# ScalarE instead of VectorE rounds the last four gelu tiles of each round of the second layer

## The chip, the cores and the metric

The kernel runs on one core of one Trainium2 chip. The metric is the time of one execution on the device in microseconds (us), lower is better. The kernel before was timed three times: median 1027.67 us, 1027.58 to 1029.29.

## The reference

Two layers work on x, (4, 512, 128) in fp32. The first one (a normalisation, a test-time-training attention of 16 heads and a mixture of 16 experts) is not touched by the change. The second one is, cut to what matters:

```
xn = layernorm(x)                               # 4 batches of 512 tokens, 128 wide
s  = q k^T / sqrt(8); e = exp(s - max(s))       # attention, 16 heads of 8, 512 x 512 each
att = (e v / sum(e)) Wo^T + bo
cur = xn
for r in range(4):                              # the mixture, four rounds one after the other
    cw  = softmax over the top 2 of (cur Wg[r] + bg[r])        # weights of 4 experts
    hmid = gelu(cur W1 + b1)                    # per expert 128 -> 512
    cur = cur + sum_e cw_e * (hmid_e W2_e + b2_e)
x = x + att + cur
```

The matrix products of the mixture keep nearly the precision of fp32: each factor is split into a high part, rounded to a shorter float format (fp32r in the profile's names), and a low part, the rest. A product is then three matmuls: high x high, low x high, high x low.

## The kernel before

Tokens of one batch are columns: a tile is 128 features x 512 tokens. The second layer runs 16 rounds, numbered R = 0 to 15 here; R = 4 i + r, i the batch and r the round of its mixture. Each round also computes four of the batch's sixteen attention heads, so that TensorE has attention work between the steps of the mixture.

Every engine has one program, in an order written out by hand; `then_inc` on an instruction counts a semaphore up and `wait_ge` makes an engine wait for a count. An engine runs its instructions strictly in that order, so whatever stands behind a waiting instruction waits too. In a round (`round_` of each engine):

TensorE: `scores(t)` (L1410) makes the attention scores of 128 keys, 4 heads, into four PSUM banks; `logits` (L1429) the gate's; `hidden(0)` to `hidden(15)` the 16 hidden tiles (4 experts x 4), three matmuls each by the helper `mm3` (L1117 to L1119); `outputs(0)` to `outputs(15)`, three matmuls each with the same helper, multiply the split gelu tiles by W2, four tiles to an expert, and the last of an expert counts `outputs_ready`; `turned(t)` (L1420) makes the scores again, turned and less their maximum, for the exp; `values(t)` (L1379) multiplies the exps with v. The end of the order is: outputs(0), (1), the turned maxima (L1484), outputs(2), (3), turned(0), outputs(4) to (6), turned(1), outputs(7), (8), values(0), turned(2), outputs(9), (10), values(1), turned(3), outputs(11) to (15), values(2), values(3). `turned(1)` needs exp 0 to be done, since both use the same four banks, and so on.

ScalarE: 16 gelus (L611), with a few small steps between them; then four exps (L626), one behind each `turned`; then one Copy of the heads' values (L597). Gelu and exp need a table load (ACT_TABLE_LOAD) between them. A gelu from the ninth on waits until the tile whose place it takes has been split: there are places for eight.

GpSimd splits tiles 0 to 11 (`POOL_TILES = 12`): L1088 rounds a tile (`hdh`), L1090 subtracts the rounded one from it (`hdl`).

VectorE: maxima of the scores (L933), gate arithmetic, then the stretch that the change touches, with what each step waits for:

```
expert(0)      # waits for outputs_ready of expert 0; L949 scales and weights, L955 adds to cur
split(12)      # L940 rounds by a multiply with ones, L943 subtracts
split(13)
expert(1)
split(14)
split(15)
expert(2)      # for r = 0 and i > 0 the division of the last batch's attention comes first
expert(3)
```

and at the start of the next round the split of `cur` (L959, L960), which its hidden tiles read. The split tiles lie in a ring of 12 places. Tile 12 takes the place of tile 0, so whoever writes `hdh` or `hdl` of tiles 12 to 15 must wait until expert 0's outputs of the same round are done (`outputs_ready`, L939 and, in the new program, on ScalarE too).

Of the kernel before, what the change touches and what calls it, by code (L numbers as in the profile page):

```python
# [7 lines left out]
ALU = mybir.AluOpType  # L8
ACT = mybir.ActivationFunctionType
AX_X = mybir.AxisListType.X  # L10

P = 128
B, S = 4, 512
# [11 lines left out]
E1, F1, R1 = 4, 512, 4  # L25
NF = F1 // P
# [37 lines left out]
def build(nc, A, out, const_d, dbg=None):  # L64
    with ExitStack() as ctx:
        def sb(name, shape, dt=F32):
            return ctx.enter_context(nc.sbuf_tensor(name, shape, dt))

        def sem(name):
            return ctx.enter_context(nc.semaphore(name))  # L70
# [116 lines left out]
        def sb(name, shape, dt=F32):  # L187
# [4 lines left out]
        RING = 3 * NF  # L192
        hdl = sb("hdl", [P, RING, S], F32R)
        hdh = sb("hdh", [P, RING, S], F32R)
        hd = [xn[:, :, :].rearrange("p (k t) d -> p k (t d)", k=4), sb("hd", [P, 4, S])]
        tile = lambda n: hd[n % 2][:, n % 8 // 2, :]
        W2h = sb("W2h", [P, E1, F1], F32R)
        W2l = sb("W2l", [P, E1, F1], F32R)
        W1r = ex[:, :, :, :].rearrange("p a q s -> p (a q) s")[:, 0:4, :]
        W2r = ex[:, :, :, :].rearrange("p a q s -> p (a q) s")[:, 4:8, :]  # L200
        W1h = sb("W1h", [P, E1, F1], F32R)
        W1l = sb("W1l", [P, E1, F1], F32R)
# [29 lines left out]
        ones2 = sb("ones2", [P, 2 * NT * E1])  # L232
# [14 lines left out]

        l2_norm_step, l2_squares = sem("l2_norm_step"), sem("l2_squares")
        xn2_turned, xn2_turned_taken, l2_w_turned, l2_w_taken, l2_w_split = sem("xn2_turned"), sem("xn2_turned_taken"), sem("l2_w_turned"), sem("l2_w_taken"), sem("l2_w_split")
        N_ROUNDS = ("xn_split", "w1_split", "w1_low", "w2_split", "pool_split", "dve_split", "cur_split", "rows_ready", "rows_high", "rows_low", "rows_placed", "v_ready", "v_taken", "scores_ready",  # L250
            "score_max", "maxima_split", "maxima_turned", "q_ready", "turned_ready", "exps_ready", "hidden_ready",
            "gelu_ready", "outputs_ready", "expert_scaled", "cur_added", "values_summed", "heads_taken", "heads_gathered", "sums_moved", "inverses_spread", "heads_divided",
            "logits_ready", "logits_taken", "logits_shifted", "gate_tanh", "gates_ready", "gates_turned", "gates_taken", "gates_stored",
            "gates_spread", "att_out", "result_ready", "result_stored")
        ROUND = {n: sem("rounds_" + n) for n in N_ROUNDS}
        moe_loaded = sem("moe_loaded")
# [158 lines left out]
        POOL_TILES = 12  # L415

        @block.scalar
        def _(act):
# [130 lines left out]
            n = 0  # L549
# [36 lines left out]
            def rows(i, k, bank_):  # L586
                n = 2 * i + 1 - k
                act.wait_ge(ROUND["rows_ready"], n + 1)
                if i:
                    act.wait_ge(ROUND["rows_placed"], 16 * 6 * R1 * i)  # L590
                act.activation(kqh[:, k, :], bank_[:, :], ACT.Copy).then_inc(ROUND["rows_high"], 1)

            def heads(R):
                act.wait_ge(ROUND["values_summed"], NT * (R + 1))
                if R:
                    act.wait_ge(ROUND["heads_gathered"], 32 * R)
                act.activation(ob[:, :], bank[5][:, :], ACT.Copy).then_inc(ROUND["heads_taken"], 1)  # L597

            def round_(R):
                i, r = divmod(R, R1)  # L600
                if R:
                    heads(R - 1)
                for n in range(E1 * NF):
                    act.wait_ge(ROUND["hidden_ready"], E1 * NF * R + n + 1)
                    if n >= 8:
                        act.wait_ge(ROUND["pool_split"], 2 * (POOL_TILES * R + n - 7))
                    elif R and n + 8 < POOL_TILES:
                        act.wait_ge(ROUND["pool_split"], 2 * (POOL_TILES * (R - 1) + n + 9))
                    elif R:
                        act.wait_ge(ROUND["dve_split"], 2 * ((E1 * NF - POOL_TILES) * (R - 1) + n + 9 - POOL_TILES))  # L610
                    act.activation(tile(n), bank[TILE_BANK[n % 3]][:, :], ACT.Gelu_apprx_tanh, bias=b1c[:, n:n + 1]).then_inc(ROUND["gelu_ready"], 1)  # L611
                    if n == 1:
                        act.wait_ge(ROUND["logits_shifted"], R + 1)
                        act.activation(half_tanh, gt[:, 0, :], ACT.Tanh, scale=0.5).then_inc(ROUND["gate_tanh"], 1)
                    if n == 7:
                        act.wait_ge(ROUND["gates_turned"], R + 1)
                        if R:
                            act.wait_ge(ROUND["gates_stored"], 16 * R)
                        act.activation(cwT[:, :], bank[7][0:E1 * NT, 0:P], ACT.Copy).then_inc(ROUND["gates_taken"], 1)
                    if n == 10 and r >= 2 and i + 1 < B:  # L620
                        rows(i + 1, 3 - r, bank[7])
                for t in range(NT):
                    act.wait_ge(ROUND["turned_ready"], NT * R + t + 1)
                    if NT * R + t >= 2:
                        act.wait_ge(ROUND["values_summed"], NT * R + t - 1)
                    act.activation(ex[:, t % 2, :, :], quad[:, :, :], ACT.Exp, scale=float(AD) ** -0.5).then_inc(ROUND["exps_ready"], 1)  # L626
# [3 lines left out]
            for R in range(B * R1):  # L630
                round_(R)
# [3 lines left out]
        def _(dve):  # L635
            n = [0]
# [261 lines left out]
            def round_(R):  # L898
# [34 lines left out]
                    dve.tensor_reduce(mx[:, t, :], quad[:, :, :], AX_X, ALU.max, negate=True).then_inc(ROUND["score_max"], 1)  # L933

                def split(n):
                    m = E1 * NF * R + n
                    dve.wait_ge(ROUND["gelu_ready"], m + 1)
                    if m >= RING:
                        dve.wait_ge(ROUND["outputs_ready"], (m - RING) // NF + 1)  # L939
                    dve.tensor_tensor(hdh[:, m % RING, :], tile(n), ones2[:, 0:1].broadcast_to([P, S]), ALU.mult).then_inc(ROUND["dve_split"], 1)  # L940
                    k = (E1 * NF - POOL_TILES) * R + n - POOL_TILES
                    dve.wait_ge(ROUND["dve_split"], 2 * k + 1)
                    dve.tensor_tensor(hdl[:, m % RING, :], tile(n), hdh[:, m % RING, :], ALU.subtract).then_inc(ROUND["dve_split"], 1)  # L943

                def expert(e):
# [34 lines left out]
                m = Mt[:, :, :].rearrange("p t (h c) -> p t h c", c=32)  # L980
# [3 lines left out]
                dve.tensor_tensor(qm[:, :], bank[7][:, :], qx[:, R % 2, :], ALU.add).then_inc(ROUND["q_ready"], 1)  # L984
                expert(0)
                split(12)
# [4 lines that stand above are left out]
                if r == 0 and i:  # L991
# [13 lines left out]
        def _(pool):  # L1005
# [70 lines left out]
            pool.memset(Mt[:, :, :], 0.0).then_inc(l2_pool_step, 1)  # L1076
            pool.memset(Vx[:, :, :, :], 0.0).then_inc(l2_pool_step, 1)
            pool.wait_ge(ROUND["w1_split"], 1)
            pool.tensor_tensor(W1l[:, :, :], W1r[:, :, :], W1h[:, :, :], ALU.subtract).then_inc(ROUND["w1_low"], 1)
            pool.wait_ge(ROUND["w2_split"], 1)  # L1080
            pool.tensor_tensor(W2l[:, :, :], W2r[:, :, :], W2h[:, :, :], ALU.subtract).then_inc(ROUND["w2_split"], 1)

# [24 lines left out]
        def _(pe):  # L1107
# [7 lines left out]
            def mm3(to, lh, ll, rh, rl, start=True, stop=True):  # L1115

                pe.matmul(to, lh, rh, start=start, stop=False, skip_group_check=True)  # L1117
                pe.matmul(to, ll, rh, start=False, stop=False, skip_group_check=True)  # L1118
                return pe.matmul(to, lh, rl, start=False, stop=stop, skip_group_check=True)  # L1119
# [199 lines left out]
            for b in range(B):  # L1319
# [3 lines left out]
                for g in range(E0 // 4):  # L1323
                    n = jobs[0]
# [68 lines left out]
            def round_(R):  # L1393
# [53 lines left out]
                def outputs(n):  # L1447
                    e, a = n // NF, n % NF
                    if a == 0 and e < 2:
                        pe.wait_ge(ROUND["gelu_ready"], E1 * NF * R + (14, 16)[e])  # L1450
                    if a == 0 and e >= 2:
                        pe.wait_ge(ROUND["expert_scaled"], E1 * R + e - 1)
                    m = E1 * NF * R + n
                    if n < POOL_TILES:
                        pe.wait_ge(ROUND["pool_split"], 2 * (POOL_TILES * R + n + 1))
                    else:
                        pe.wait_ge(ROUND["dve_split"], 2 * ((E1 * NF - POOL_TILES) * R + n - POOL_TILES + 1))
                    c = slice(a * P, (a + 1) * P)
                    last = mm3(bank[6 if e % 2 else 4][:, :], W2h[:, e, c], W2l[:, e, c], hdh[:, m % RING, :], hdl[:, m % RING, :], start=(a == 0), stop=(a == NF - 1))
                    if a == NF - 1:  # L1460
                        last.then_inc(ROUND["outputs_ready"], 1)
# [43 lines left out]
                if R == 0:  # L1505
                    pe.wait_ge(ROUND["w2_split"], 2)
                outputs(0), outputs(1)
                turn_maxima()
                outputs(2), outputs(3), turned(0), outputs(4), outputs(5), outputs(6), turned(1), outputs(7), outputs(8)
                values(R, 0), turned(2), outputs(9), outputs(10), values(R, 1), turned(3), outputs(11)  # L1510
                if R < LAST:
                    outputs(12), outputs(13), outputs(14), outputs(15), values(R, 2), values(R, 3)
# [3 lines left out]
            rows(0, 1, bank[1])  # L1516
            rows(0, 0, bank[0])
            pe.wait_ge(xn2_turned_taken, B)
            pe.wait_ge(ROUND["w1_low"], 1)
            for R in range(B * R1):  # L1520
                round_(R)
            attention_out(B - 1)
# [28 lines left out]
```

## Time and profile before

| | before |
|---|---|
| median of 3 runs | 1027.67 us |
| profiled execution | 1030.62 us |
| its span | 1028.7 us |
| TensorE busy | 929.5 us, 90% |
| VectorE busy | 832.1 us, 81% |
| GpSimd busy | 626.5 us, 61% |
| ScalarE busy | 557.7 us, 54% |

The span is the time from the first to the last instruction of the profiled execution. The second layer's rounds fill it from about 442 us to about 1010 us; one round is about 35 us. A line of the timeline gives start, duration, engine, line of the program, operation, output and input names, a count where several were merged, and in brackets the idle time of the engine just before it, with what ended it. Names: PE is TensorE, DVE VectorE, ACT ScalarE, POOL GpSimd; the x tiles `xn` and `hd` hold the gelus, `ex` the exps, `quad` is four PSUM banks.

### The profile page before, as it was taken

The numbers are of one execution on the slowest core, as the hardware profiler recorded it, in microseconds if no ns is written. First come the engines' busy times: TensorE is split into PE (matmuls) and PEld (weight loads), VectorE is DVE, ScalarE is ACT, GpSimd is POOL, SyncE is SP. The second block draws the span as 40 slices with busy tenths as digits, with TensorE's granted clock in tenths as the row PEclk, the third lists the DMA queues.
The fourth block names the chain that finished last, engine by engine and source line by source line (L and its number), as shares of the span: only waits on it lengthen the run. The fifth ranks groups of instructions, "written<-read, shape, count | busy, mean of one in ns | idle before, by whom it ended". The sixth has DMA issues, their size and how long they took to land.

```text
span 1028.7 us, 16635 instructions
## 1 busy us (share of the span) xinstructions
PE 929.5 (90%) x6216; PEld 651.3 (63%) x6216; DVE 832.1 (81%) x1276; ACT 557.7 (54%) x826; POOL 626.5 (61%) x575
## 2 busy tenths in 40 slices
PE   2688899999999789779999999999999999999993
PEld 1456678778787667755565566656656666566552
DVE  7778999998998752678888888888897888878882
ACT  3334555555555436254666565657656666666560
POOL 5464666666666300195966696678668766866690
PEclk9989999999999989989999999999999999999997
DMA  8000000000000030220110122011111111121010
GB/s 223 16 1 1 2 1 1 2 1 1 2 2 2 1 82 2 82 72 6 55 59 13 52 69 70 19 42 60 62 30 53 60 45 29 60 71 34 30 41 26
DMA packets 25006, 38.13 MB, mean 37 GB/s; under 512 B 9336, under 2 KB 15500, under 8 KB 22880
## 3 DMA queue, kind: packets, MB, share of 16 engines
q1 hardware_dynamic: 23296, 34.81, 11.2%
q10 hardware_dynamic: 1632, 2.27, 0.7%
q8 instruction: 50, 0.82, 0.3%
q14 instruction: 28, 0.23, 0.1%
HBM read 28.29 MB, written 1.44 MB: 29 GB/s over the span
## 4 chain that ended last, share of the span: by engine, by line
PE 54%; POOL 18%; DVE 13%; issue 8%; ACT 5%; DMA 1%; SPq 1%; POOLq 0%; ACTq 0%; DVEq 0%
POOL hdl L1090 10%; PE bank L1117 9%; PE bank L1119 7%; PE bank L1118 7%; PE quad L1158 5%; PE bank L1379 5%; POOL hdh L1088 4%; PE bank L1268 3%; PE quad L1243 3%; ACT ex L626 2%; PE quad L1152 2%; PE quad L1420 2%; PE quad L1315 1%; PE bank L1208 1%; PE bank L1350 1%
## 5 line engine op out<-in xcount | busy, mean ns | idle before, releaser
L933 DVE TENSOR_REDUCE mx<-quad 128x4 f32<-128x2048 f32 x64 | 146.3, 2286 | 40.1 <-PE quad L1410 40.0
L1088 POOL CAST hdh<-xn 128x512 fp32r<-128x512 f32 x96 | 66.3, 690 | 143.7 <-ACT xn L611 143.7
L626 ACT ACTIVATE ex<-quad 128x2048 f32<-128x2048 f32 x64 | 120.6, 1884 | 50.1 <-PE quad L1420 49.9
L1090 POOL TENSOR_TENSOR hdl<-hd,hdh 128x512 fp32r<-128x512 f32 x96 | 129.7, 1351 | 7.7
L1090 POOL TENSOR_TENSOR hdl<-xn,hdh 128x512 fp32r<-128x512 f32 x96 | 128.8, 1341 | 7.7
L611 ACT ACTIVATE hd<-bank,b1c 128x512 f32<-128x512 f32 x128 | 88.1, 688 | 64.0 <-POOL hdl L1090 33.5
L1117 PE MATMUL bank<-hdh,W2h 128*128 128x512 f32 x256 | 111.3, 435 | 2.7 <-DVE hdl L943 2.7
L611 ACT ACTIVATE xn<-bank,b1c 128x512 f32<-128x512 f32 x128 | 87.9, 687 | 34.3 <-POOL hdl L1090 19.5
L1119 PE MATMUL bank<-hdl,W2h 128*128 128x512 f32 x256 | 101.0, 395 | 0.0
L1118 PE MATMUL bank<-hdh,W2l 128*128 128x512 f32 x256 | 100.7, 393 | 0.0
L1117 PE MATMUL bank<-cH,W1h 128*128 128x512 f32 x192 | 81.2, 423 | 0.7 <-DVE cL L960 0.7
L1119 PE MATMUL bank<-cL,W1h 128*128 128x512 f32 x192 | 75.8, 395 | 0.0
L1118 PE MATMUL bank<-cH,W1l 128*128 128x512 f32 x192 | 75.6, 394 | 0.0
L1088 POOL CAST hdh<-hd 128x512 fp32r<-128x512 f32 x96 | 70.3, 732 | 0.0
L1117 PEld LDWEIGHTS bank<-hdh,W2h 128*128 128x128 f32 x256 | 48.0, 188 | 32.8 <-issue 11.4
L1158 PE MATMUL quad<-Wbd,arena 128*64 128x128 f32 x1024 | 67.3, 285 | 0.0
L1379 PE MATMUL bank<-ex,Vx 128*32 128x512 f32 x512 | 65.5, 605 | 0.0
L1049 POOL TENSOR_TENSOR arena<-arena,sm 128x512 f32<-128x512 f32 x32 | 33.4, 1044 | 52.1 <-DVE sm L774 52.1
L955 DVE TENSOR_TENSOR cur<-cur,add 128x512 f32<-128x512 f32 x60 | 62.2, 1036 | 2.1
L1158 PEld LDWEIGHTS quad<-Wbd,arena 128*64 128x64 f32 x1024 | 58.1, 142 | 6.8 <-issue 6.6
L1037 POOL TENSOR_TENSOR arena<-arena,gg 128x512 f32<-128x512 f32 x32 | 40.9, 1279 | 31.2 <-DVE arena L751 30.4
L949 DVE SCALAR_TENSOR_TENSOR add<-bank,b2T,cwB 128x512 f32<-128x512 f32 x64 | 47.7, 746 | 14.2 <-PE bank L1119 14.0
(295 smaller groups left out, 2275.4 us busy)
## 6 DMA issues: line engine op xcount, KB each, us to landing
cwB<-gate_rows SPq DMA_DIRECT2D x16, 1024.0 KB, 4.7
kx<-kqh SPq DMA_DIRECT2D x32, 64.0 KB, 2.1
qx<-kqh SPq DMA_DIRECT2D x32, 64.0 KB, 2.1
ex<-in_L_ffn_W SPq DMA_DIRECT2D x1, 1024.0 KB, 5.4
kx<-kql SPq DMA_DIRECT2D x16, 64.0 KB, 2.1
qx<-kql SPq DMA_DIRECT2D x16, 64.0 KB, 2.1
num<-ob SPq DMA_DIRECT2D x16, 64.0 KB
rec<-rec_rows SPq DMA_DIRECT2D x32, 32.0 KB, 2.1
```

The source lines that it names most:

```text
L611: act.activation(tile(n), bank[TILE_BANK[n % 3]][:, :], ACT.Gelu_apprx_tanh, bias=b1c[:, n:n + 1]).then_inc(ROUND["gelu_ready"], 1)
L626: act.activation(ex[:, t % 2, :, :], quad[:, :, :], ACT.Exp, scale=float(AD) ** -0.5).then_inc(ROUND["exps_ready"], 1)
L933: dve.tensor_reduce(mx[:, t, :], quad[:, :, :], AX_X, ALU.max, negate=True).then_inc(ROUND["score_max"], 1)
L949: dve.scalar_tensor_tensor(out=add[:, e % 2, :], in0=bank[6 if e % 2 else 4][:, :], scalar=b2T[:, e:e + 1], in1=cwB[:, e, :], op0=ALU.add, ...
L955: dve.tensor_tensor(now, before, add[:, e % 2, :], ALU.add).then_inc(ROUND["cur_added"], 1)
L1088: pool.tensor_copy(hdh[:, m % RING, :], tile(n)).then_inc(ROUND["pool_split"], 1)
L1090: pool.tensor_tensor(hdl[:, m % RING, :], tile(n), hdh[:, m % RING, :], ALU.subtract).then_inc(ROUND["pool_split"], 1)
L1117: pe.matmul(to, lh, rh, start=start, stop=False, skip_group_check=True)
L1118: pe.matmul(to, ll, rh, start=False, stop=False, skip_group_check=True)
L1119: return pe.matmul(to, lh, rl, start=False, stop=stop, skip_group_check=True)
L1158: last = pe.matmul(to[64 * k:64 * k + 64, a * P:(a + 1) * P], T[:, 4 * hf + a, 2 * g + k, :], Wbd[:, 2 * g + k, 4 * hf + a, :], start=Fals ...
L1379: last = pe.matmul(bank[5][32 * h:32 * h + 32, :], Vx[:, t, QH * r + h, :], ex[:, t % 2, h, :], start=(t == 0), stop=(t == NT - 1), skip_g ...
```

## The change

ScalarE gets a loop between its 16 gelus and its four exps, in which it rounds tiles 12 to 15 (an activation Copy into `hdh`) and counts a new semaphore, `act_high`. VectorE's `split` loses its multiply and waits for `act_high` instead; it only subtracts. `dve_split` therefore counts 1 per tile instead of 2, and the waits on it are divided by two. The semaphores `w1_low` and `w1_split` are made one, with the same order.

```
@@ ScalarE, round_ (the waits on dve_split, here and on TensorE, are halved) @@
+                for n in range(POOL_TILES, E1 * NF):
+                    m = E1 * NF * R + n
+                    act.wait_ge(ROUND["gelu_ready"], m + 1)
+                    if m >= RING:
+                        act.wait_ge(ROUND["outputs_ready"], (m - RING) // NF + 1)
+                    act.activation(hdh[:, m % RING, :], tile(n), ACT.Copy).then_inc(ROUND["act_high"], 1)
                 for t in range(NT):
                     act.wait_ge(ROUND["turned_ready"], NT * R + t + 1)
@@ VectorE, round_ @@
                 def split(n):
-                    m = E1 * NF * R + n
+                    m, k = E1 * NF * R + n, (E1 * NF - POOL_TILES) * R + n - POOL_TILES
                     dve.wait_ge(ROUND["gelu_ready"], m + 1)
                     if m >= RING:
                         dve.wait_ge(ROUND["outputs_ready"], (m - RING) // NF + 1)
-                    dve.tensor_tensor(hdh[:, m % RING, :], tile(n), ones2[:, 0:1].broadcast_to([P, S]), ALU.mult).then_inc(ROUND["dve_split"], 1)
-                    k = (E1 * NF - POOL_TILES) * R + n - POOL_TILES
-                    dve.wait_ge(ROUND["dve_split"], 2 * k + 1)
+                    dve.wait_ge(ROUND["act_high"], k + 1)
                     dve.tensor_tensor(hdl[:, m % RING, :], tile(n), hdh[:, m % RING, :], ALU.subtract).then_inc(ROUND["dve_split"], 1)
```

## Rows read from the trace of the kernel before

**Rows 1.** The page, its first part: busy time, share of the span, instructions.

```profile
PE 929.5 (90%) x6216; PEld 651.3 (63%) x6216; DVE 832.1 (81%) x1276; ACT 557.7 (54%) x826; POOL 626.5 (61%) x575
```

**Rows 2.** The page, the chain that ended last, by engine.

```profile
PE 54%; POOL 18%; DVE 13%; issue 8%; ACT 5%; DMA 1%; SPq 1%; POOLq 0%; ACTq 0%; DVEq 0%
```

**Rows 3.** The waits, TensorE from 400 us: us in total, times, longest.

```profile
PE quad L1420 <- ACT ex L626: 7.7, 9, 0.9
...
PE bank L1117 <- DVE hdl L943: 2.7, 3, 2.0
```

**Rows 4.** The timeline, ScalarE, round 7: last gelu to exp 0.

```profile
712.77 0.69 ACT L611 ACTIVATE hd<-bank,b1c 128x512 f32<-128x512 f32 x1 [1.24 <-POOL hdl L1090]
713.48 1.28 ACT L626 ACT_TABLE_LOAD   x1
714.77 1.88 ACT L626 ACTIVATE ex<-quad 128x2048 f32<-128x2048 f32 x1
```

**Rows 5.** The timeline, TensorE, round 7: turned(1), outputs(14), next hidden(0).

```profile
716.70 0.51 PE L1420 MATMUL quad<-qm,kx 32*128 32x512 f32 x4 [0.86 <-ACT ex L626]
...
725.36 0.39 PE L1117 MATMUL bank<-hdh,W2h 128*128 128x512 f32 x1
...
730.01 0.48 PE L1117 MATMUL bank<-xH,W1h 128*128 128x512 f32 x1
```

**Rows 6.** Groups of instructions: count, busy us, mean ns, idle before.

```profile
L940 DVE TENSOR_TENSOR hdh<-hd,ones 128x512 fp32r<-128x512 f32 x32 | 30.5, 952 | 0.0
...
L591 ACT ACTIVATE kqh<-bank 128x512 fp32r<-128x512 f32 x6 | 3.6, 600 | 3.8 <-PE bank L1119 3.8
...
L574 ACT ACTIVATE arena<-xn 128x512 f32<-128x512 f32 x4 | 2.5, 630 | 19.4 <-DVE xn L846 19.4
```

**Rows 7.** The timeline, VectorE, round 7: expert(0).

```profile
713.17 0.75 DVE L949 SCALAR_TENSOR_TENSOR add<-bank,b2T,cwB 128x512 f32<-128x512 f32 x1 [0.71 <-PE bank L1119]
```

**Rows 8.** The timeline, three engines, round 9.

```profile
784.70 1.28 ACT L626 ACT_TABLE_LOAD   x1
785.99 1.89 ACT L626 ACTIVATE ex<-quad 128x2048 f32<-128x2048 f32 x1
...
785.22 0.75 DVE L949 SCALAR_TENSOR_TENSOR add<-bank,b2T,cwB 128x512 f32<-128x512 f32 x1 [0.70 <-PE bank L1119]
...
787.93 0.51 PE L1420 MATMUL quad<-qm,kx 32*128 32x512 f32 x4
```

**Rows 9.** The timeline, three engines, round 8.

```profile
749.88 1.89 ACT L626 ACTIVATE ex<-quad 128x2048 f32<-128x2048 f32 x1 [0.62 <-PE quad L1420]
...
749.43 0.75 DVE L949 SCALAR_TENSOR_TENSOR add<-bank,b2T,cwB 128x512 f32<-128x512 f32 x1 [0.71 <-PE bank L1119]
...
747.36 0.63 PE L1484 MATMUL bank<-cst,Mt 128*128 128x128 f32 x4 [1.52 <-DVE Mt L982]
...
752.02 0.51 PE L1420 MATMUL quad<-qm,kx 32*128 32x512 f32 x4
...
766.75 0.48 PE L1117 MATMUL bank<-cH,W1h 128*128 128x512 f32 x1 [0.22 <-DVE cL L960]
```

**Rows 10.** The timeline, TensorE, round 0: turned(1), outputs(14), next hidden(0).

```profile
468.77 0.51 PE L1420 MATMUL quad<-qm,kx 32*128 32x512 f32 x4
...
479.57 0.53 PE L1117 MATMUL bank<-hdh,W2h 128*128 128x512 f32 x1 [1.99 <-DVE hdl L943]
...
486.07 0.49 PE L1117 MATMUL bank<-cH,W1h 128*128 128x512 f32 x1
```

**Rows 11.** The timeline, TensorE, first layer.

```profile
61.69 0.50 PE L1152 MATMUL quad<-Bhl,pair 4*128 4x512 f32 x1 [2.39 <-DVE arena L751]
```

**Rows 12.** Stretches, TensorE: us, busy (count), granted clock, DMA share, GB/s.

```profile
63.00:66.00 3.00, 3.00 (x26) 0.58 0.00 0
481.00:484.00 3.00, 3.00 (x15) 0.61 0.00 0
749.00:752.00 3.00, 3.00 (x15) 1.00 0.18 51
```

More of the change, by code:

```diff
@@ L249, in build @@
         xn2_turned, xn2_turned_taken, l2_w_turned, l2_w_taken, l2_w_split = sem("xn2_turned"), sem("xn2_turned_taken"), sem("l2_w_turned"), sem("l2_w_taken"), sem("l2_w_split")
-        N_ROUNDS = ("xn_split", "w1_split", "w1_low", "w2_split", "pool_split", "dve_split", "cur_split", "rows_ready", "rows_high", "rows_low", "rows_placed", "v_ready", "v_taken", "scores_ready",
+        N_ROUNDS = ("xn_split", "w1_split", "w2_split", "pool_split", "act_high", "dve_split", "cur_split", "rows_ready", "rows_high", "rows_low", "rows_placed", "v_ready", "v_taken", "scores_ready",
             "score_max", "maxima_split", "maxima_turned", "q_ready", "turned_ready", "exps_ready", "hidden_ready",
@@ L609, in round_ @@
                     elif R:
-                        act.wait_ge(ROUND["dve_split"], 2 * ((E1 * NF - POOL_TILES) * (R - 1) + n + 9 - POOL_TILES))
+                        act.wait_ge(ROUND["dve_split"], (E1 * NF - POOL_TILES) * (R - 1) + n + 9 - POOL_TILES)
                     act.activation(tile(n), bank[TILE_BANK[n % 3]][:, :], ACT.Gelu_apprx_tanh, bias=b1c[:, n:n + 1]).then_inc(ROUND["gelu_ready"], 1)
@@ L1078, in _ @@
             pool.wait_ge(ROUND["w1_split"], 1)
-            pool.tensor_tensor(W1l[:, :, :], W1r[:, :, :], W1h[:, :, :], ALU.subtract).then_inc(ROUND["w1_low"], 1)
+            pool.tensor_tensor(W1l[:, :, :], W1r[:, :, :], W1h[:, :, :], ALU.subtract).then_inc(ROUND["w1_split"], 1)
             pool.wait_ge(ROUND["w2_split"], 1)
@@ L1456, in outputs @@
                     else:
-                        pe.wait_ge(ROUND["dve_split"], 2 * ((E1 * NF - POOL_TILES) * R + n - POOL_TILES + 1))
+                        pe.wait_ge(ROUND["dve_split"], (E1 * NF - POOL_TILES) * R + n - POOL_TILES + 1)
                     c = slice(a * P, (a + 1) * P)
@@ L1518, in _ @@
             pe.wait_ge(xn2_turned_taken, B)
-            pe.wait_ge(ROUND["w1_low"], 1)
+            pe.wait_ge(ROUND["w1_split"], 2)
             for R in range(B * R1):
```

## The prediction

> **What bounds the kernel now.** I read the page first. TensorE is busy for 929.5 of the 1028.7 us [rows 1], and the chain that ended last lies on it for 54%, on GpSimd for 18%, on VectorE for 13%, on ScalarE for only 5% [rows 2]. So TensorE is the engine to lose time on; the 5% of ScalarE asks where its links of the chain sit, since the change gives work to exactly that engine. The table of waits answers it: from 400 us on, TensorE's matmuls of the second attention product (`turned`, L1420) stood 7.7 us in 9 waits of about 0.86 us for an exp, while its waits for VectorE's split tiles come to 2.7 us in all [rows 3]. VectorE's rounding, which the change takes away, hardly holds anything up; the exp does.
>
> Then I laid round 7 out by engine (16 rounds, 0 to 15; 9 of them, 1 to 3, 6, 7, 10, 11, 14 and 15, look alike). The last gelu runs from 712.77 to 713.46, the table load of exp follows at once, and exp 0 runs from 714.77 to 716.65 [rows 4]. TensorE has issued the outputs that it may and starts `turned(1)` at 716.70, 0.86 us late [rows 5]. From there it works without a listed idle to the first hidden tile of the next round at 730.01, which is 13.31 us [rows 5]. The gelus of that round wait for that tile, so a delay of exp 0 is not made good.
>
> **The change, part by part.** *Removed:* 4 multiplies (L940) a round on VectorE, 0.95 us each by their mean [rows 6], 3.8 us a round and 61 us over the kernel. VectorE is not what TensorE waits for here; this is worth nothing in the alike rounds.
>
> *Added, the copies:* 4 copies of 128x512 from SBUF to SBUF on ScalarE. The trace of before has no such Copy; the nearest is the Square of the same size between SBUF tiles, 0.63 us [rows 6]. Bounds: 0.60, a Copy of that size out of PSUM [rows 6], and 0.69, the gelu [rows 4]. I take 0.63, so 4 x 0.63 = 2.52 us. They stand behind the last gelu and ahead of the exps, so behind them queue the table load and the four exps, and behind those TensorE's `turned` and `values`.
>
> *Added, their waits:* the gelu they read is done. The other wait is for expert 0's outputs of this very round, `outputs(3)`. VectorE's L949 starts on the same event, at 713.17 [rows 7]: before the gelu ends at 713.46, so it costs nothing in the alike rounds. There exp 0 ends 2.52 later and TensorE's wait grows from 0.86 to 3.38: 9 x 2.52 = 22.7 us.
>
> In rounds 5, 9 and 13 the outputs are later. In round 9 the table load starts at 784.70 behind the last gelu and the exp at 785.99, but L949 only starts at 785.22, so the copies start then, 0.5 later than the load did [rows 8]. Exp 0 moves by 0.5 + 2.52 = 3.0. `turned(1)` at 787.93 followed exp 0's end (787.88) at once [rows 8], so all of it lands: 3 x 3.0 = 9.1 us.
>
> In rounds 4, 8 and 12 exp 0 waited for `turned(0)` and the table load lay under that wait. Round 8: the outputs at 749.43, then 2.52 of copies and 1.28 of load, so exp 0 at 753.2 where it was at 749.88, 3.3 later; `turned(1)` at 752.02 had 0.2 of room behind its end at 751.77 [rows 9], so it moves 3.1. But in these rounds the stretch from `turned(1)` to the next round's first hidden tile is 752.02 to 766.75, 14.73 us [rows 9], against 13.31 in round 7: VectorE was late, with the splits in its queue. Without the multiplies that 1.4 goes. Net 1.7; 3 x 1.7 = 5.1 us (round 8 stands for the three).
>
> Round 0 is such a one too: 17.30 us from 468.77 to 486.07 [rows 10], of which 4.0 can come back against 3.1 of delay: -0.9 us. I charge the other splits nothing: behind a TensorE that is 2.5 us later, VectorE's subtracts, fed by the copies from about 714.1, end well ahead of the outputs that read them. Sum: 22.7 + 9.1 + 5.1 - 0.9 = 36.0 us.
>
> *Added, the clock:* this is the second cost, and it comes from the length of the new stalls. After an idle of 1.99 us at 479.57 [rows 10], and of 2.39 us at 61.69 [rows 11], the granted clock of the stretches behind was 0.61 and 0.58, so mostly at 1.2 GHz; behind 1.52 us idle at 747.36 it stayed at 1.00, that is 2.4 GHz [rows 9, 12]. The 0.86 us of today does no harm; 3.0 to 3.4 us in every round are above every case that did. The price at a drop: from `outputs(14)` to the next hidden tile it took 479.57 to 486.07, 6.50 us, against 725.36 to 730.01, 4.65, in round 7 [rows 5, 10]: 1.85 us. Some of the slow time may fall into the stall itself and cost nothing, so I take 1.5, with 0 and 1.85 as ends: 16 x 1.5 = 24 us. The clock's slow stretch lies behind `turned(1)`, in TensorE's own work, and nothing covers it.
>
> The Trainium skill, "TensorE: Matmul & The Clock Gate" (§ The HAM clock gate), says that activity releases the throttle and that an engine idle for long enough falls back to the half rate; by its figures the stalls worked out here fall short of a full idle stretch, and the clock would stay up. The 1.99 us of round 0 already speaks against reading it so. By the skill's rule the sum is 36, by the rows 60.
>
> Total: 36 + 24 = 60 us. The profiled execution took 1030.62 us (span 1028.7), so it would be 1090.7; the median of the runs is 1027.67, 2.95 below the profiled one, and the forecast against it is 1088 us.
>
> **Rivals.**
> A. The clock stays up: the new stalls are single ones in dense work, and where the drops were seen it may have been something else in their neighbourhood that let the clock fall. For it: rows 11 and the first of rows 12 lie in the first layer, where TensorE is less busy. Against: 1.99 us in round 0 of this very loop was enough. 1027.7 + 36 = 1064 us.
> B. The drops last longer: a second slow stretch in each round, as the half rate makes TensorE late and further waits follow. 16 x 2 x 1.5 = 48 instead of 24: 1112 us.
> C. The other side, faster: ScalarE's share of the chain is small and VectorE's late splits are the true brake. Its place are the late stretches of rounds 0, 4, 8 and 12, its price 4.0 + 3 x 1.4 = 8.2 us, 1019 us. It decides only if exp 0 had 2.5 us of room ahead of `turned(1)`; the rows show 0.2 us in round 8 and none in 7 and 9.
> D. The delay is mostly absorbed (TensorE finds later work to catch up on): about 1040 us. Against it stands that 13.31 us hold no idle.
>
> **How the numbers follow.** Forecast 0.73, A 0.16, B 0.05, C 0.02, D 0.04. The forecast's own range is 1078 to 1096 (copies of 0.60 to 0.69 us: -2 to +4; drops of 1.0 to 1.85 each: -8 to +6; not all at their ends together). The 8 in 10 take in A: 1061 to 1097. This kernel's measurement tells about 0.2%, 2 us, from no change. Faster 0.02, within it 0.01, slower 0.97.
>
> **What would show it.** Of the new profile: 64 ScalarE copies of about 0.63 us between L611 and L626; TensorE's waits for L626 at `turned(1)` at about 3.4 us in most rounds, some 50 us in total instead of 7.7; the alike rounds 2.5 us longer without, about 4 with the clock; granted clock near 0.5 for some 3 us behind each such wait, so page digits of 8 or 9 where a 9 stood; VectorE's busy time down by about 61 us or more. The prediction is wrong if exp 0 starts 1.3 us behind the last gelu as today, if the waits are there but the clock holds (A), or if the alike rounds grow by more than 5 us (B).

## The result and the profile after

The changed kernel takes 1090.55 us (median of 4 runs, 1086.8 to 1091.3) against 1028.1 us of the kernel before: 1.060 times as long, interval 1.057 to 1.063. The forecast was 1088 us.

The lines that answer to [rows 1 to 3]: the page's busy times and its chain, and, from 400 us on, TensorE's waits (us in total, times, longest).

```profile
PE 952.7 (87%) x6216; PEld 661.8 (61%) x6216; DVE 760.8 (70%) x1212; ACT 591.4 (54%) x890; POOL 613.4 (56%) x575
```

```profile
PE 59%; POOL 14%; DVE 11%; ACT 10%; issue 4%; DMA 1%; SPq 1%; ACTq 0%; POOLq 0%; DVEq 0%
```

```profile
PE quad L1424 <- ACT ex L632: 46.5, 16, 3.1
```

VectorE is 71.3 us lighter (61 for the multiplies, most of the rest for its adds to `cur`, 0.83 us each by their mean where they were 1.04), and nothing is gained by it. ScalarE's share of the chain doubled. The wait at `turned` was 7.7 us in 9 places and is 46.5 us in 16. TensorE has the same 6216 matmuls as before and is busy 23.2 us longer with them, so they ran slower.

Round 7 on ScalarE, for [rows 4]:

```profile
737.64 0.69 ACT L611 ACTIVATE hd<-bank,b1c 128x512 f32<-128x512 f32 x1 [1.24 <-POOL hdl L1094]
738.23 0.62 ACT L627 ACTIVATE hdh<-xn 128x512 fp32r<-128x512 f32 x1
738.75 0.62 ACT L627 ACTIVATE hdh<-hd 128x512 fp32r<-128x512 f32 x1
739.27 0.62 ACT L627 ACTIVATE hdh<-xn 128x512 fp32r<-128x512 f32 x1
739.79 0.62 ACT L627 ACTIVATE hdh<-hd 128x512 fp32r<-128x512 f32 x1
740.43 1.28 ACT L632 ACT_TABLE_LOAD   x1
741.72 1.88 ACT L632 ACTIVATE ex<-quad 128x2048 f32<-128x2048 f32 x1
```

From the end of the last gelu (738.33) to exp 0 it is 3.39 us, where it was 1.31: 2.08 us more. The copies last 0.62 us each, but start 0.52 us apart, and the first starts 0.10 us before the gelu has ended. The same round on TensorE, for [rows 5], and its stretches (busy us, count, granted clock, DMA share, GB/s):

```profile
743.65 0.80 PE L1424 MATMUL quad<-qm,kx 32*128 32x512 f32 x4 [2.92 <-ACT ex L632]
...
749.11 0.80 PE L1424 MATMUL quad<-qm,kx 32*128 32x512 f32 x4
...
759.67 0.48 PE L1121 MATMUL bank<-xH,W1h 128*128 128x512 f32 x1
```

```profile
740.00:743.00 3.00, 0.73 (x4) 1.00 0.00 0
743.00:746.00 3.00, 2.35 (x8) 0.50 0.00 0
746.00:749.00 3.00, 3.00 (x12) 0.50 0.00 0
749.00:752.00 3.00, 3.00 (x22) 0.86 0.00 0
```

`turned(1)` waits 2.92 us, and behind it the clock is at half, 1.2 GHz, for some six microseconds. From `turned(1)` to the next hidden tile it is 16.02 us instead of 13.31. Not all rounds are like that: against the 13.3 us that this stretch takes at full clock, eight lose about 1.5 us, six (3, 4, 7, 8, 10 and 15, the last by its length beside experiment 1) about 2.7, and two, 12 and 13, nothing. Round 12, `turned(1)` and the next hidden tile, 13.32 us apart, and the stretch behind the idle:

```profile
942.18 0.51 PE L1424 MATMUL quad<-qm,kx 32*128 32x512 f32 x4 [2.82 <-ACT ex L632]
...
955.50 0.48 PE L1121 MATMUL bank<-cH,W1h 128*128 128x512 f32 x1
```

```profile
942.00:948.00 6.00, 5.82 (x36) 1.00 0.00 0
```

### The profile page after: what moved, and what is told of

Read it like the earlier page. It is cut to its first block, busy times and chain, and to the rows that moved or that the text cites. A ratio compares the mean times of both kernels' runs of the same rounds, so it can differ in the third digit from the quotient of the medians.

```text
span 1089.3 us, 16699 instructions
## 1 busy us (share of the span) xinstructions
PE 952.7 (87%) x6216; PEld 661.8 (61%) x6216; DVE 760.8 (70%) x1212; ACT 591.4 (54%) x890; POOL 613.4 (56%) x575
## 4 chain that ended last, share of the span: by engine, by line
PE 59%; POOL 14%; DVE 11%; ACT 10%; issue 4%; DMA 1%; SPq 1%; ACTq 0%; POOLq 0%; DVEq 0%
PE bank L1121 10%; POOL hdl L1094 9%; PE bank L1123 8%; PE bank L1122 8%; PE bank L1383 6%; PE quad L1162 5%; POOL hdh L1092 4%; ACT ex L632 3%; PE bank L1272 3%; ACT hdh L627 2%; PE quad L1424 2%; PE quad L1247 2%; ACT L632 2%; PE quad L1156 2%; PE bank L1212 1%
## 5 line engine op out<-in xcount | busy, mean ns | idle before, releaser
L1094 POOL TENSOR_TENSOR hdl<-hd,hdh 128x512 fp32r<-128x512 f32 x96 | 127.3, 1326 | 7.7
L1094 POOL TENSOR_TENSOR hdl<-xn,hdh 128x512 fp32r<-128x512 f32 x96 | 125.6, 1309 | 7.7
L1121 PE MATMUL bank<-hdh,W2h 128*128 128x512 f32 x256 | 116.8, 456 | 0.0
L1123 PE MATMUL bank<-hdl,W2h 128*128 128x512 f32 x256 | 106.6, 416 | 0.0
L1122 PE MATMUL bank<-hdh,W2l 128*128 128x512 f32 x256 | 106.4, 415 | 0.0
L611 ACT ACTIVATE xn<-bank,b1c 128x512 f32<-128x512 f32 x128 | 87.9, 687 | 32.7 <-POOL hdl L1094 19.4
L1424 PE MATMUL quad<-qm,kx 32*128 32x512 f32 x256 | 37.1, 570 | 46.5 <-ACT ex L632 46.5
L1383 PE MATMUL bank<-ex,Vx 128*32 128x512 f32 x512 | 72.7, 665 | 0.0
L1424 PEld LDWEIGHTS quad<-qm,kx 32*128 32x128 f32 x256 | 13.8, 206 | 93.2 <-ACT ex L632 68.4
L1121 PEld LDWEIGHTS bank<-hdh,W2h 128*128 128x128 f32 x256 | 51.1, 200 | 31.4 <-issue 17.9
L1092 POOL CAST hdh<-hd 128x512 fp32r<-128x512 f32 x96 | 64.8, 675 | 0.0
L1053 POOL TENSOR_TENSOR arena<-arena,sm 128x512 f32<-128x512 f32 x32 | 33.4, 1044 | 52.1 <-DVE sm L780 52.1
```

The lines of the kernel that those rows point to most:

```text
L1092: pool.tensor_copy(hdh[:, m % RING, :], tile(n)).then_inc(ROUND["pool_split"], 1)
L1094: pool.tensor_tensor(hdl[:, m % RING, :], tile(n), hdh[:, m % RING, :], ALU.subtract).then_inc(ROUND["pool_split"], 1)
L1383: last = pe.matmul(bank[5][32 * h:32 * h + 32, :], Vx[:, t, QH * r + h, :], ex[:, t % 2, h, :], start=(t == 0), stop=(t == NT - 1), skip_g ...
L1424: last = pe.matmul(quad[:, h, :], kx[rows_, R % 2, t * P:(t + 1) * P], qm[rows_, :], start=True, stop=True)
```

## The experiments

Seven kernels, each timed four times or five; one execution of each is profiled. In the table "loop" is the span of the profiled execution less the start of the first gelu, since the part ahead of it, which nothing here touches, differs by up to 3 us from run to run (442.45 to 445.5).

| | median us | ratio to before (interval) | loop us |
|---|---|---|---|
| before | 1028 to 1029 | 1 | 583.95 |
| changed | 1090.55 | 1.060 (1.057 to 1.063) | 643.80 |
| fillers in the stall | 1060.81 | 1.032 (1.031 to 1.034) | 616.65 |
| copies added, nothing removed | 1088.44 | 1.059 (1.057 to 1.062) | 640.93 |
| multiplies removed, no copies | 1022.42 | 0.995 (0.994 to 0.997) | 577.16 |
| copies between the exps | 1022.91 | 0.995 (0.993 to 0.997) | 577.40 |
| one copy ahead of the exps | 1037.29 | 1.008 (1.006 to 1.010) | 591.2 |
| two copies | 1060.11 | 1.030 (1.026 to 1.033) | 614.8 |
| three copies | 1071.91 | 1.041 (1.038 to 1.044) | 627.4 |

**1. Is it the idle that lets the clock fall?** TensorE gets work for the stall.

```
+                def filler():
+                    for k in range(10):
+                        pe.matmul(bank[7][:, :], W1h[:, 0, 0:P], high, start=True, stop=True, skip_group_check=True)
...
-                outputs(2), outputs(3), turned(0), outputs(4), outputs(5), outputs(6), turned(1), outputs(7), outputs(8)
+                outputs(2), outputs(3), turned(0), outputs(4), outputs(5), outputs(6), filler(), turned(1), outputs(7), outputs(8)
```

> The changed kernel, with ten more matmuls (512 columns each) on TensorE just ahead of turned(1), into a PSUM bank that nobody reads before it is written anew. Ten of them take about 2.2 us at the pace of 0.22-0.23 us in the rows, less than the 2.8 to 3.1 us for which TensorE waits there in the changed kernel, so they delay nothing and leave an idle of some 0.7 us. Theory (the idle stretch lets the clock fall, and the half clock behind it is the second cost): granted clock 1.00 through the rounds, and the time falls by the sum of the excess of the stretches from turned(1) to the next hidden tile, about 29 us: 1062 us (1058 to 1066). Rival (the clock falls for another cause, or the long stretches come from VectorE's and ScalarE's new order): stays at 1088 to 1091 us.

It took 1060.81 us. Round 7 of it, and the stretch around the fillers:

```profile
725.79 2.50 PE L1479 MATMUL bank<-cH,W1h 128*128 128x512 f32 x10
728.88 0.51 PE L1424 MATMUL quad<-qm,kx 32*128 32x512 f32 x4 [0.59 <-ACT ex L632]
```

```profile
726.00:729.00 3.00, 2.41 (x14) 1.00 0.00 0
```

Exp 0 is as late as in the changed kernel (3.39 us behind the last gelu in the alike rounds), the idle is 0.59 us, and behind `turned(1)` the clock holds in all 16 rounds. So the cost is two costs: 616.65 - 583.95 = 32.7 us is the delay of exp 0, and 643.80 - 616.65 = 27.2 us is the clock, brought down by the idle and by nothing else that the change does, since all the rest of it is still in. The rival is out.

Round 0 blurs the border between the two by about 1.4 us. With the fillers it begins with a stretch at half clock that the changed kernel has not. It lies 5.5 us behind the first gelu, long before the fillers, and the two rows show that place in both:

```profile
448.00:452.00 4.00, 4.00 (x13) 0.57 0.32 81
```

```profile
451.00:455.00 4.00, 3.86 (x20) 1.00 0.31 76
```

The first is the kernel with the fillers, the second the changed one. So round 0 is 42.15 us long there and 42.32 here, although only the latter has a fall behind `turned(1)`. Added up over the 14 rounds with a fall, the stretches behind `turned(1)` are 28.6 us longer than at full clock (round 15 by its length), and that leaves about 31 us for the delay.

**2. Does the removal give anything back?** VectorE multiplies again, behind the copies, with the same values.

```
                     dve.wait_ge(ROUND["act_high"], k + 1)
+                    dve.tensor_tensor(hdh[:, m % RING, :], tile(n), ones2[:, 0:1].broadcast_to([P, S]), ALU.mult).then_inc(ROUND["dve_split"], 1)
+                    dve.wait_ge(ROUND["dve_split"], 2 * k + 1)
```

> Addition alone: ScalarE makes its four copies as in the changed kernel, and VectorE still makes its four multiplies behind them (it writes the same values once more), so nothing is removed. Theory (the copies' delay of exp 0 and the clock are all of the cost; VectorE's multiplies lie beside a later TensorE): as the changed kernel, 1088 to 1094 us. Rival (the removal of the multiplies gives 8 us back in rounds 0, 4, 8 and 12, as the prediction's sum has it): 1098 us.

1088.44 us: its interval and the changed kernel's overlap almost wholly. The clock falls in 13 of its 16 rounds. Rounds 8 and 12 happen to keep it and take 38.21 and 38.22 us, where with the fillers and without the multiplies they take 38.23 and 38.22. The multiplies are free as soon as exp 0 is late.

**3. The removal alone.** The copies' loop and VectorE's wait for it are left out of the changed kernel.

```
-                for n in range(POOL_TILES, E1 * NF):
...
-                    act.activation(hdh[:, m % RING, :], tile(n), ACT.Copy).then_inc(ROUND["act_high"], 1)
...
-                    dve.wait_ge(ROUND["act_high"], k + 1)
```

> Removal alone: no copies on ScalarE and no multiplies on VectorE (the high parts of tiles 12 to 15 are what lay in the ring before, so the kernel leaves their rounding out). Theory: VectorE's multiplies only hold TensorE up in rounds 0, 4, 8 and 12; about 2 us come back in round 0 (0.7 of the stall, and the half clock behind it), 1.4 in rounds 4 and 8, 0.4 in round 12: 5 to 6 us faster than before, 1022 to 1024 us. Rival (VectorE is a brake in all rounds): 4 x 0.95 us in 16 rounds, down to 970 us; or nothing at all, 1028 us.

1022.42 us, 0.5% faster than before. The gain sits in the rounds where it was expected, but is larger in round 0 than the 2 us forecast: it is 38.81 us long instead of 42.31; rounds 4 and 8 are 1.4 us shorter, round 12 is 0.4 us shorter, and no other moves by more than 0.1. In round 0 the stall of `outputs(14)`, 1.99 us in [rows 10], is 0.56, and the half clock behind it is gone:

```profile
477.97 0.50 PE L1114 MATMUL bank<-hdh,W2h 128*128 128x512 f32 x1 [0.56 <-DVE hdl L940]
```

**4. The copies in ScalarE's own gaps.** Tile 12 behind exp 0, 13 and 14 behind exp 1, 15 behind exp 2.

```
                     act.activation(ex[:, t % 2, :, :], quad[:, :, :], ACT.Exp, scale=float(AD) ** -0.5).then_inc(ROUND["exps_ready"], 1)
+                    for n in ((12,), (13, 14), (15,), ())[t]:
...
+                        act.activation(hdh[:, m % RING, :], tile(n), ACT.Copy).then_inc(ROUND["act_high"], 1)
```

> The copies moved off the path: tile 12 behind exp 0, tiles 13 and 14 behind exp 1, tile 15 behind exp 2, where ScalarE waits 0.6, 1.15 and 1.13 us for the next turned scores in round 7. The copies follow one another at 0.52 us in the changed kernel's trace, so they fit. Theory (only the place ahead of exp 0 costs): the delay and the clock's fall both go, and the gain of the removal stays: 1022 to 1026 us, faster than both kernels. Rival (any copy among the exps is paid in full, 0.5 us or more of each gap, for it drags the next exp): 1028 + 16 x 1 = 1044 us or more.

1022.91 us, faster than both kernels. ScalarE in round 7 of it, and TensorE's waits for the exps from 450 us on:

```profile
708.22 1.28 ACT L626 ACT_TABLE_LOAD   x1
709.51 1.88 ACT L626 ACTIVATE ex<-quad 128x2048 f32<-128x2048 f32 x1
711.29 0.62 ACT L632 ACTIVATE hdh<-xn 128x512 fp32r<-128x512 f32 x1
712.01 1.89 ACT L626 ACTIVATE ex<-quad 128x2048 f32<-128x2048 f32 x1
713.78 0.62 ACT L632 ACTIVATE hdh<-hd 128x512 fp32r<-128x512 f32 x1
714.30 0.62 ACT L632 ACTIVATE hdh<-xn 128x512 fp32r<-128x512 f32 x1
715.00 1.88 ACT L626 ACTIVATE ex<-quad 128x2048 f32<-128x2048 f32 x1
716.78 0.61 ACT L632 ACTIVATE hdh<-hd 128x512 fp32r<-128x512 f32 x1
```

```profile
PE quad L1424 <- ACT ex L626: 7.6, 9, 0.9
```

Exp 0 to exp 1 is 2.50 us, as it was before (714.77 to 717.26); the copy lies in the gap. TensorE's wait is back at 7.6 us in 9 places. The copies, their count and the removal are those of the changed kernel: only the place differs, and it is worth 67.6 us. Against the removal alone there is nothing between them that these runs can tell.

**5 to 7. The dose.** ScalarE rounds only the first one, two or three of the four tiles ahead of the exps (`ACT_TILES` = 1, 2, 3), and VectorE multiplies the others.

```
-                for n in range(POOL_TILES, E1 * NF):
+                for n in range(POOL_TILES, POOL_TILES + ACT_TILES):
```

One copy:

> Dose: ScalarE rounds only tile 12 ahead of the exps, VectorE keeps the multiplies of tiles 13 to 15. By the changed kernel's trace a copy takes 0.52 us of ScalarE's time. In the alike rounds exp 0 moves by 0.52 us (9 x 0.52 = 4.7), in rounds 5, 9 and 13 by the wait for the outputs and the copy (1.24, 1.24, 1.5: 4.0), in 0, 4, 8 and 12 by 1.3 against what comes back: about 0. Idle ahead of turned(1) 1.2 to 1.5 us. Theory (the clock depends on the idle's length, and 1.5 us did not bring it down before): clock 1.00, 1036 us (1033 to 1040). Rival (any lengthening of the stall brings the clock down): 22 us more, 1058.

Two copies:

> Dose: tiles 12 and 13 on ScalarE. Without the clock 15 x 0.52 = 8 us more than with one tile, 1044 us; idle ahead of turned(1) about 1.9 us, between the 1.52 that left the clock alone and the 1.99 that did not. Theory: some of the rounds drop, so between 1044 and 1066, I take 1052. Rival (the copies alone, no clock): 1044.

Three copies:

> Dose: tiles 12 to 14 on ScalarE. Without the clock 1052 us; idle ahead of turned(1) about 2.4 us, as long as the 2.39 in the first layer behind which the clock fell. Theory: most rounds drop at 1.5 us each, 1072 us (1064 to 1078). Rival (the clock needs the 2.8 us and more of the changed kernel): 1052.

1037.29, 1060.11 and 1071.91 us. `turned(1)` of round 1 with one copy, then the stretch behind its idle:

```profile
506.27 0.50 PE L1430 MATMUL quad<-qm,kx 32*128 32x512 f32 x4 [1.35 <-ACT ex L634]
```

```profile
506.00:509.00 3.00, 2.73 (x18) 1.00 0.00 0
```

With two copies, rounds 1 and 2, and a stretch behind each:

```profile
507.55 0.51 PE L1430 MATMUL quad<-qm,kx 32*128 32x512 f32 x4 [1.89 <-ACT ex L634]
...
544.63 0.51 PE L1430 MATMUL quad<-qm,kx 32*128 32x512 f32 x4 [1.88 <-ACT ex L634]
```

```profile
510.00:513.00 3.00, 3.00 (x15) 0.62 0.01 3
...
544.00:547.00 3.00, 2.37 (x14) 1.00 0.00 0
```

With three, round 1:

```profile
508.54 0.80 PE L1430 MATMUL quad<-qm,kx 32*128 32x512 f32 x4 [2.39 <-ACT ex L634]
```

```profile
508.00:511.00 3.00, 2.46 (x8) 0.60 0.00 0
```

Each copy moves exp 0 by 0.52 us (1.83, 2.35, 2.87 and, in the changed kernel, 3.39 us behind the last gelu in the alike rounds). The clock comes on top: it falls in none of the 16 rounds with one copy (idle 1.3 to 1.4 us), in 10 with two (1.8 to 1.9), in 12 with three (2.3 to 2.4), in 14 with four (2.8 to 3.1), each counted in one profiled execution. Less its clock, each case lies near the line 1036, 1044, 1052, 1061: the step of 23 us from one copy to two is 8 us of copy and 10 falls at 1.5 us. The forecast of two copies, 1052, was too low for this reason: more rounds fell than I had allowed for, but within its stated 1044 to 1066.

## Why the prediction was right, step by step

**The bound.** TensorE's wait at `turned(1)` in [rows 3] marked the place where a delay is paid in full. It was: with the fillers the alike rounds are 2.07 us longer by their mean (round 7: 36.59 against 34.54), and exp 0's delay is 2.08.

**The copies.** The term was 2.52 us a round, and it measured 2.08. The duration was right (0.62 against 0.63 us), but I multiplied durations where the starts are 0.52 us apart. The Trainium skill, "ScalarE: Activation LUTs" (§ What ACT_TABLE_LOAD costs), says that back-to-back ACTIVATEs overlap by about 93 ns; the 0.10 us between the copies here agree. Nine rounds gave 18.7 us instead of 22.7.

**Rounds 5, 9 and 13.** 9.1 us forecast; with the fillers they are 2.8, 3.1 and 2.8 longer, 8.7 us. The copies are shorter than forecast, but the first one stands 0.6 to 0.9 us behind the last gelu for the outputs, where I had read off 0.5 from one round.

**Rounds 4, 8 and 12.** 5.1 us forecast, 5.5 measured with the fillers (1.5, 1.5 and 2.5; round 12 was late by 0.4 us only, so round 8 did not stand for it). The size was right and the reason was not: I let the delay be offset by the removal of the multiplies. Experiment 2 keeps the multiplies, and its rounds 8 and 12, which kept the clock, have the same lengths. What offsets it is that TensorE, being later, no longer meets VectorE's lateness. The removal has a gain of its own only where no copies delay exp 0 (experiment 3).

**Round 0.** -0.9 us forecast, -0.2 measured with the fillers, whose round 0 has the extra stretch at half clock. The changed kernel's, less its fall, is 40.8 us, 1.5 less than before; so this term stays open by about 1.3 us. Experiment 2 has the multiplies, the extra stretch and a long fall of 2.7 us in round 0 and takes 44.85 us, which is 42.15 without the fall, as with the fillers: here too the multiplies cost nothing once exp 0 is late.

**The clock.** 24 us forecast as 16 falls at 1.5 us; 27.2 us measured as 14 falls, eight at about 1.5 and six at about 2.7. The price of one fall was right for the common case. That the half clock would at times last twice as long was the size of rival B, which I applied to all rounds or none; it came in six. It came without B's mechanism: in the 16.02 us of round 7 no further wait is listed, the half rate itself lasted longer. The reading of the Trainium skill, "TensorE: Matmul & The Clock Gate" (§ Part 1: The HAM clock gate), by which such stalls would leave the clock alone is not borne out here: it fell behind 14 stalls of 2.8 to 3.1 us. The two errors, the copies' 4 us too much and the clock's 3 us too little, nearly cancel: 60 us forecast, 59.9 in the loop. That they cancel is luck, but either alone would have moved the forecast by 4 us at most, within its range. (1030.62 + 60 is 1090.6, not 1090.7; the forecast does not hang on it.)

**The rivals.** A (clock stays up, 1064) is what the fillers make of the kernel, 1060.81. C (faster) has the right sign for the removal, 5.5 us instead of 8 (its price took 1.4 us for round 12 too, which had 0.4 to give), but its condition, room ahead of `turned(1)`, is only met when the copies stand elsewhere. D is out: nothing but the lateness of rounds 0, 4, 8 and 12 absorbs any of it.

## What to carry to other kernels

Busy share does not say where spare time is: ScalarE was the least loaded of the four engines, and the 2.1 us put on it ahead of exp 0 cost 62 us, while the same four copies a few instructions later cost nothing that could be measured. Before work is moved to an idle engine, look for the gap in its own timeline that is to take it, and for who waits behind that place. And where a stall of the matrix engine grows, price the clock beside it: here it nearly doubled the bill, and from one copy to two it cost more than the copy.

## What the runs showed of the hardware

The clock's fall behind an idle is not decided by its length alone. An idle of 1.89 us brought it down and one of 1.88 us, a round later in the same execution, did not; 2.82 us did not in rounds 12 and 13 of the changed kernel, and 2.83 us did in round 8. Across the four doses the share of rounds that fall rises from 0 to 10, 12 and 14 of 16. The widest overlap lies in experiment 2: its round 9 idled for 3.11 us and kept the clock, while with two copies 1.78 us (round 13) lost it. Round 9, and the stretch behind it:

```profile
820.23 0.51 PE L1426 MATMUL quad<-qm,kx 32*128 32x512 f32 x4 [3.11 <-ACT ex L632]
```

```profile
820.00:823.00 3.00, 2.77 (x18) 1.00 0.00 0
```

The time at half rate came in two sizes, worth about 1.5 and 2.7 us, and which of them it is goes with the moment of the fall. Of the 49 falls in the four kernels with falls, 11 were long; in those TensorE was still idle when the clock fell, 0.34 to 0.80 us ahead of `turned(1)`. In the 38 short ones it fell between 0.20 us ahead of `turned(1)` and 1.7 us behind its start. Round 7 of the changed kernel is a long one, and its clock is at half ahead of `turned(1)` at 743.65:

```profile
743.20:743.60 0.40, 0.00 (x0) 0.50 0.00 0
```

What sets the moment, and whether the clock falls at all, was not tried. Nor is it shown that this makes a kernel's time scatter: the runs spread from 1086.5 to 1091.7 us with four copies, from 1055.7 to 1062.7 with two and from 1060.3 to 1061.2 with the fillers, but those of the kernel before, whose profile has no fall behind a `turned(1)`, from 1027.2 to 1031.0 as well.
